# Gated delta-net attention and channel mixing on one core: three steps of the recurrence woven instead of two, heads of four batches exchanged, part of a triangular solve moved to GpSimd

## The reference, cut to what matters

```
q, k = l2norm(silu(conv4(x @ W.T)))        # 16 heads, 64 wide
v    = silu(conv4(x @ Wv.T))               # 16 heads, 128 wide
alpha = exp(-exp(A_log) * softplus(x @ Wa.T + dt_bias)); beta = 2*sigmoid(x @ Wb.T)
for t in range(1024):                      # per batch and head
    S = alpha_t * (S - beta_t * k_t (k_t S)) + k_t v_t
    o_t = S q_t
out = rmsnorm(o) @ Wo.T
```

## Time and profile before

| | |
|---|---|
| median of 3 runs | 4767.3 us (4766.52 to 4771.13) |
| profiled execution | 4768.39 us, its span 4766.6 us |
| mean granted TensorE clock | 0.932 of 2.4 GHz |
| busy in the span | PE 3981.9 us, DVE 3447.9, ACT 2826.5, POOL 1620.0 |
| one engine's list once round (KT of step 0 to KT of step 127, over 127) | 34.67 us |

### The profile page before, as it was taken

How to read it: one execution, slowest core, us unless ns; L and a number is a source line. 1 busy time by engine, 2 the same in 40 slices (tenths; PEclk the granted TensorE clock), 3 DMA queues, 4 the chain that set the end, 5 groups by cost and what they waited for, 6 DMA issues and landing times. The chain is left out here.

```text
span 4766.6 us, 171733 instructions
## 1 busy us (share of the span) xinstructions
PE 3981.9 (84%) x67980; PEld 2818.1 (59%) x67980; DVE 3447.9 (72%) x7448; ACT 2826.5 (59%) x4519; POOL 1620.0 (34%) x1574
## 2 busy tenths in 40 slices
PE   5888888888888888888888888888888888888855
PEld 4565665656666565666666565666656566666644
DVE  5777777777777777777777777777777777777745
ACT  2666656666565656656665666656565665666534
POOL 2333333333333333333333333333333333333311
PEclk9999999999999999999999999999999999999977
DMA  1211111121211112121111111121111212111111
GB/s 53 44 38 42 39 38 41 39 43 39 43 38 40 41 37 42 39 43 38 41 40 37 42 39 43 39 42 38 38 43 37 43 39 43 38 41 40 36 39 40
DMA packets 877987, 191.80 MB, mean 40 GB/s; under 512 B 816000, under 2 KB 873600, under 8 KB 877952
## 3 DMA queue, kind: packets, MB, share of 16 engines
q1 hardware_dynamic: 871648, 173.49, 17.3%
q0 software_dynamic: 6304, 17.84, 1.3%
HBM read 136.16 MB, written 55.06 MB: 40 GB/s over the span
## 5 line engine op out<-in xcount | busy, mean ns | idle before, releaser
L830 DVE SCALAR_TENSOR_TENSOR cv<-ps,w_v,cv 128x512 f32<-128x512 f32 x768 | 576.6, 751 | 562.7 <-ACT cv L695 544.6
L830 DVE SCALAR_TENSOR_TENSOR cv<-ps,w_kq,cv 128x512 f32<-128x512 f32 x768 | 575.2, 749 | 139.9 <-ACT cv L695 121.8
L695 ACT ACTIVATE cv<-ps,w_kq 128x512 f32<-128x512 f32 x256 | 175.9, 687 | 623.0 <-PE ps L449 623.0
L502 PE MATMUL ps<-k_all,KB 64*64 64x64 f32 x4096 | 225.4, 289 | 326.3 <-issue 326.3
L460 PE MATMUL ps<-Lm,k_all 128*128 128x512 f32 x768 | 418.5, 626 | 0.0
L997 POOL TENSOR_TENSOR sq<-sl 128x512 f32<-128x512 f32 x128 | 133.0, 1039 | 838.6 <-ACT sl L710 838.6
L990 POOL COPY stP<-tabP 128x24 f32 (+1 forms) x128 | 25.3, 197 | 1144.1 <-DVE KT L859 1144.1
L502 PEld LDWEIGHTS ps<-k_all,KB 64*64 64x64 f32 x4096 | 206.2, 197 | 340.0 <-issue 340.0
L469 PE MATMUL ps<-sq,k_all 128*128 128x512 f32 x512 | 285.1, 639 | 138.6 <-ACT ex L702 138.6
L710 ACT ACTIVATE sl<-cv 128x512 f32<-128x512 f32 x256 | 161.5, 631 | 369.8 <-DVE cv L830 369.8
L449 PE MATMUL ps<-xnT,w_v 128*128 (+1 forms) x1024 | 298.2, 412 | 98.8 <-DVE Nd L845 53.0
(11 more groups left out here) (184 smaller groups left out, 10890.3 us busy)
## 6 DMA issues: line engine op xcount, KB each, us to landing
scrN<-Nd SPq DMA_DIRECT2D x256, 128.0 KB, 2.4
Z<-scrZ SPq DMA_DIRECT2D x256, 128.0 KB, 2.8
X<-scrX SPq DMA_DIRECT2D x512, 64.0 KB
w_v<-wtab SPq DMA_DIRECT2D x128, 132.0 KB, 2.1
w_kq<-wtab POOLq DMA_DIRECT2D x128, 132.0 KB, 2.4
wo_s<-wo SPq DMA_DIRECT2D x128, 128.0 KB, 2.4
NS<-scrN SPq DMA_DIRECT2D x128, 64.0 KB, 2.5
scrZ<-XT SPq DMA_DIRECT2D x128, 64.0 KB, 2.5
```

Source lines behind the costliest of these rows:

```text
L502: last = nc.tensor.matmul(sub_block(ps, 6 * 512, b, a, z), sub_block(BD["KB"], 0, b, a, z), k_all[a:z, K_ID + a:K_ID + z], start=True, sto ...
L695: nc.scalar.activation(cv4[:, j], pj[:, :, 0:C], ACT.Copy, scale=tap(j, 0)).then_inc(tap0.sem, 1)
L830: nc.vector.scalar_tensor_tensor(cv4[:, j], pj[:, :, k:k + C], tap(j, k), cv4[:, j], ALU.mult, ALU.add).then_inc(conv.sem, 1)
```

## The change

It does these things.

- **Three steps woven.** `body(l, m, n)` with m = l + 1 and n = l + 2: output, state update and second inverse round of l; SiLU of v, inverse and first round, ks and R of m; projections, keys and decay factors of n. There is one more partly filled round at each end.
- **Heads exchanged for batches 4 to 7.** "Class 1" batches keep their token tensors (V, R, U, the decay of the tables) with the two heads' partitions exchanged (`place`, `other`), so that in both Grams, ktr, ks, ds, y, x and z class 0 uses two quadrants and class 1 the other two. u keeps two. The exchange is made in the tables, in `wab` and by the output pattern of the SiLU of v (`sv_out`).
- **Decay factors.** `pe_decay`'s three 128x512 products become eight 64x64x256 ones (`pe_dec`), one exp of 1024 columns writes both factors. exp(g) for all steps is written once, ahead of the steps, to HBM (scrG), and SyncE reads a step's rows repeated over 64 partitions (`sp_g`, two DMAs).
- **Substitution on GpSimd.** `pool_elim`, 14 instructions of up to 32 elements in a row, replaces numbers 0 to 12 of `dve_sub`; VectorE keeps five.
- w_kq is issued by SyncE instead of GpSimd. ScalarE's list changes its function table four times in a round instead of twice. The S part and the U part of o are split by a wait for class 1.

The lists of the round, and what the prediction's steps use:

```diff
-SUBS = 18
+ELIM = 14
+SUBS = 5
+        def sp_g(sp, n):
+            if not first(n):
+                sp.wait_ge(qg_ok.sem, qg_ok.at(n - 1))
+            for h, (a, z) in enumerate(HALF):
+                sp.dma_start(half(ex, 2)[a:z], scrG[bass.ds(n, 1), h, :].to_broadcast([C, NB * C])).then_inc(g_in.sem, 16)
+        def sp_inv_out(sp, n):
+            sp.wait_ge(sub.sem, sub.at(n, SUBS - 1))
+            sp.dma_start(blocks(scrZ), X16).then_inc(z_out.sem, 16)
+            sp.wait_ge(sub.sem, sub.at(n))
+            sp.dma_start(blocks(scrX), XB[0:64, :]...).then_inc(x_out.sem, 16)
+        def sp_body(sp, m, n, q):          # called with (i, i+1, i+2), as the others with (l, m, n)
+            if q is not None:
+                sp_wkq(sp, q)
+            sp_gram(sp, n)
+            if m is not None:
+                sp_wo(sp, m)
+            if q is not None:
+                sp_wv(sp, q)
+                sp_g(sp, q)
+            sp_inv_out(sp, n)
+            sp_inv_in(sp, n)
+        def pool_qg(pool, n):
+            pool.wait_ge(qn_ok.sem, qn_ok.at(n))
+            pool.wait_ge(g_in.sem, g_in.at(n))
+            if not first(n):
+                pool.wait_ge(o_mm.sem, o_mm.at(n - 1))
+            nc.gpsimd.tensor_tensor(half(BD["QG"], 0), qn[:], half(ex, 2), ALU.mult).then_inc(qg_ok.sem, 1)
+        def pool_elim(pool, n):
+            if not first(n):
+                pool.wait_ge(z_out.sem, z_out.at(n - 1))
+                pool.wait_ge(sub.sem, sub.at(n - 1))
+            pool.sem_inc(pool_go.sem, 1)
+            nc.gpsimd.tensor_copy(XT[0:64, 0:256], k_all[0:64, K_XI:K_XI + 256]).then_inc(elim.sem, 1)
+            pool.wait_ge(n_in.sem, n_in.at(n))
+            for k in range(7):
+                r, c = 7 - k, k + 1
+                pool.wait_ge(elim.sem, elim.at(n, max(2 * k, 1)))
...
+                    nc.gpsimd.tensor_tensor(t, NB8[...], XB8[...], ALU.mult).then_inc(elim.sem, 1)
+                    pool.wait_ge(elim.sem, elim.at(n, 2 * k + 1))
+                    nc.gpsimd.tensor_tensor(XB8[:, :, 0:c, c:8], XB8[:, :, 0:c, c:8], t, ALU.add).then_inc(elim.sem, 1)
+        pe_body(l, m, n), with "part(step)":
+            gram_k(m) proj3(m) y1(l) x(l) z1(l) nq(m) u(l) proj0(n) o(l) ds(l) ms(l) ktr(m) proj1(n)
+            gram_p(m) ks(m) vtr(m) nk(n) wo(l) proj2(n) dec(n) y0(m) z0(m)
+        act_body: silu_v0(m) u1(l) tap0_0(n) TABLE nq_ln(m) osq(l) osq(l) nq_exp(m) o_ln, o_exp(l) twice TABLE
+            silu_v1(m) tap0_1(n) silu_k(n) sq_k(n) v(m) nk_max(n) TABLE nk_ln(n) tap0_2(n) nk_exp(n) y0(m)
+            exp(n) TABLE silu_q(n) y1(m) x(m) tap0_3(n) z1(m) nq_max(n) u0(m)
+        dve_body: conv3(m) conv0(n) s(l) s(l) sub 0-3(m) k(m) on(l) on(l) p(m) sub 4(m) conv1(n) r(m) acc(l)
+            conv2(n, two) keys(n) conv2(n, last) z0(m) n(n) str(n)
+        pool_body: qg(l) nm(l) dmn(m) sq_q(m) elim(m) dmp(m) qn(m) stp(n) lm(n) sg(m)
```

More of the change, by code:

```diff
@@ L463, in pe_norm, with pe_dec @@
[L463 to L467, removed]
-                pe.wait_ge(pt_ok.sem, pt_ok.at(n - 1))
-            nc.tensor.matmul(bank((2, 6)[i]), kc(K_BD), half(sq, i), start=True, stop=True).then_inc(nrm_mm.sem, 1)
+        def pe_dec(pe, n):
+            pe.wait_ge(lm_ok.sem, lm_ok.at(n))
+            if not first(n):
+                pe.wait_ge(r_ok.sem, r_ok.at(n - 1))
+            pe.sem_inc(pe_go.sem, 1)
+            for i, o in enumerate((K_LE, K_GT)):
+                for cls in range(2):
+                    for a, z in HALF:
+                        c = (PAIR_C + cls) * 512 + i * 4 * C
+                        last = nc.tensor.matmul(ps[place(cls, a), c:c + 4 * C], k_all[a:z, o + a:o + z],
+                                                Lm[a:z, i * 512 + cls * 4 * C:i * 512 + (cls + 1) * 4 * C], start=True, stop=True)
+            last.then_inc(dec_mm.sem, 1)
@@ L496, in pe_ktr, with pe_vtr @@
             else:
+                pe.wait_ge(nq_mx.sem, nq_mx.at(n))
                 pe.wait_ge(dec_ex.sem, dec_ex.at(n))
-                pe.wait_ge(nrm_mx.sem, nrm_mx.at(n))
             pe.sem_inc(pe_go.sem, 1)
[L500 to L503, removed]
-            last.then_inc(k_tr.sem, 1)
[L506 to L509, removed]
+            for i in range(4):
+                for cls in range(2):
+                    for a, z in HALF:
+                        last = nc.tensor.matmul(ps[place(cls, a), col64(PAIR_C, cls, i)], blk64(BD["KB"], CLASSES[cls][i], a),
+                                                k_all[a:z, K_ID + a:K_ID + z], start=True, stop=True)
+            last.then_inc(k_tr.sem, 1)
+        def pe_vtr(pe, m):
+            pe.wait_ge(silu_v.sem, silu_v.at(m))
+            if not first(m):
+                pe.wait_ge(on_ok.sem, on_ok.at(m - 1))
+            else:
+                pe.wait_ge(g_cp.sem, g_cp.at(0))
             for b in range(NB):
@@ L512, in pe_vtr, with pe_y @@
             last.then_inc(v_tr.sem, 1)
[L515 to L530, removed]
+        def pe_y(pe, m, n, l):
             if l:
-                pe.wait_ge(y_ok.sem, y_ok.at(m, 1))
+                pe.wait_ge(z_ok.sem, z_ok.at(m, 1))
             else:
@@ L558, in pe_z @@
             pe.sem_inc(pe_go.sem, 1)
[L559 to L566, removed]
+            for i in range(4):
+                for cls in range(2):
+                    for a, z in HALF:
+                        b = CLASSES[cls][i]
+                        q = place(cls, a)
+                        last = nc.tensor.matmul(ps[a:z, col64((PAIR_B, PAIR_A)[l], cls, i)],
+                                                BD["X" if l else "X0"][q, b * C:(b + 1) * C],
+                                                BD["Y"][q, b * C:(b + 1) * C], start=True, stop=True)
             last.then_inc(z_mm.sem, 1)
         def pe_ks(pe, m):
-            pe.wait_ge(kb_ok.sem, kb_ok.at(m))
             pe.wait_ge(kt_ok.sem, kt_ok.at(m))
@@ L741, in act_x, with act_v @@
+        def act_v(act, m):
+            act.wait_ge(v_tr.sem, v_tr.at(m))
+            if not first(m):
+                act.wait_ge(r_ok.sem, r_ok.at(m - 1))
+            nc.scalar.activation(Vt[:], bank(PAIR_B, 2), ACT.Copy).then_inc(v_ok.sem, 1)
         def act_x(act, m):
             act.wait_ge(x_mm.sem, x_mm.at(m))
[L743 removed]
+            if not first(m):
+                act.wait_ge(z_mm.sem, z_mm.at(m - 1))
+            nc.scalar.activation(two(half(BD["X"], 0)), pair(PAIR_A), ACT.Copy).then_inc(x_ok.sem, 1)
@@ new lines, in act_u, with act_osq @@
+        def act_u(act, m, g):
+            act.wait_ge(u_mm.sem, u_mm.at(m, g + 1))
+            if first(m):
+                act.wait_ge(g_tr.sem, g_tr.at(0))
+            else:
+                act.wait_ge(ds_mm.sem, ds_mm.at(m - 1))
+            nc.scalar.activation(half(U, g), bank(PAIR_C + g), ACT.Copy).then_inc(u_ok.sem, 1)
+        def act_osq(act, m, h):
+            act.wait_ge(o_mm.sem, o_mm.at(m))
+            if not first(m):
+                act.wait_ge(wo_mm.sem, wo_mm.at(m - 1))
+            nc.scalar.activation(half(oo, h), bank(PAIR_B + h), ACT.Square).then_inc(o_sq.sem, 1)
@@ new lines, in sp_inv_in @@
+        def sp_inv_in(sp, n):
+            sp.wait_ge(z_out.sem, z_out.at(n))
+            if not first(n):
+                sp.wait_ge(u_mm.sem, u_mm.at(n - 1))
+            for h, (a, z) in enumerate(HALF):
+                sp.dma_start(v3(BD["Z"], 0)[a:z], rows(scrZ, h)).then_inc(z_in.sem, 16)
+            sp.wait_ge(x_out.sem, x_out.at(n))
+            if not first(n):
+                sp.wait_ge(x_ok.sem, x_ok.at(n - 1))
+            for h, (a, z) in enumerate(HALF):
+                sp.dma_start(v3(BD["X0"], 0)[a:z, 0:4], rows(scrX, h)[:, 0:4]).then_inc(x_in.sem, 16)
+                sp.dma_start(v3(BD["X0"], 0)[other(a), 4:8], rows(scrX, h)[:, 4:8]).then_inc(x_in.sem, 16)
```

869 lines of the change are left out of this document (473 added, 396 removed).

## The result

| | before | after |
|---|---|---|
| median us | 4766.95 (4766.52 to 4771.13, 4 runs) | 5142.51 (5142.01 to 5142.74, 4 runs) |
| span of the profiled execution | 4766.6 | 5140.9 |
| KT to KT, over 127 | 34.67 | 37.56 |
| outside the 127 rounds | 363.1 | 370.3 |

What follows compares the result with a forecast made beforehand. The prediction took a ring through SyncE's wait for QG as the bound: 34.3 us plus 1.3 for clock and 0.5 for port made 36.1 us a round, 4958 us in all; range 4700 to 5200, forecast's own 4830 to 5110.

Steps and rivals of the forecast that it cites:

- the wait for QG ahead of the store: On SyncE: g loads wait for POOL's QG, holding back the inverse's store; QG ready 6.35 us after KT.
- the ring: Chain of waits across engines closing over one step, from KT's end to the next; 34.3 us before two additions.
- the third rival: Elimination on GpSimd is the bound: 13 small instructions take 8.7 us, total 5182 us; chance 0.15.
- The first rival: SyncE's wait for QG is not last; PE and ACT set a 28.3 us round, total 3967 us; chance 0.05.
- The second rival: TensorE keeps 2.4 GHz, no port conflicts, g loads cost no queue time: round 33.8 us, total 4665 us; chance 0.16.
- the clock: TensorE's clock falls after idling ahead of z0, slowing z0, gram_k and proj3: 1.3 us a round, between 0 and 2.5.
- the port: VectorE's sub 0 may wait for GpSimd's dmp and qn at SBUF: 0.5 us a round, up to 1.27.
- outside the rounds: Work before and after the 127 rounds: exp(g) preparation and a longer last step, +9 us, 0 to 20.
- Terms 1 and 2: From KT's end: POOL's stP, Lm, Sg and QG, 6.35 us, then SyncE issuing two g loads, 0.7 us.
- Terms 3 and 4: From the scrZ issue to X landed for z0, 8.5 us, plus g loads' traffic on the queue, 0.5 us.
- Term 6: Second inverse round, from the end of copy Z to the start of u: 4.9 us.

Runs made afterwards that it cites:

- e1: The changed kernel, but SyncE asks for the exp(g) rows after the inverse's two stores and six loads; 4132.79 us, ratio 0.8674 to the kernel before.
- e2: The changed kernel with SyncE's order kept, but POOL multiplies QG(m) right behind qn(m), not first in its next round; 4161.29 us, ratio 0.8734 to before.
- e7: e1 with POOL's qn(m) made to wait until VectorE's sub 0 to 2 are done; 4045.43 us, ratio 0.8482 to before.
- e8: e7 with VectorE making the transposed copy XB (sub 4) right behind KT(m); 3901.75 us, ratio 0.818 to before.
- e5: The changed kernel with eight unused products added on TensorE, six ahead of y0 and two between y0 and z0; 5047.66 us, ratio 1.0581 to before.
- e4: The changed kernel, but POOL's qn(m) waits until VectorE's sub 0 to 2 are done; 5137.85 us, ratio 1.0783 to before.
- e3: The changed kernel with five unused products added on TensorE between dec(n) and y0(m); 5143.63 us, ratio 1.0795 to before.

## Why the prediction was right, and what its sizes missed

The mechanism was right: the wait for QG ahead of the store closes the ring, and e1 and e2 remove it in two ways. The size was not: it came out at half of the measured one, 191 of 376 us. The measured 5142.5 us lie above the forecast's own 4830 to 5110. They are inside 4700 to 5200 only by the room left for the third rival, the elimination as the bound, and that is not what happened. To that extent the range held by luck.

The first rival, that this wait is not last, is refuted by e1 and e2. Its 28.3 us, the round of PE and ACT alone, is near what is left without the wait (e1 29.62, e7 28.96), but no floor: e8 has 27.81. The second rival failed as the clock fell and the port bit in every one of the 115 rounds. The third failed as the small instructions on GpSimd took 0.20 to 0.26 us and 0.31 apart, 4.0 in all where I had 5.5.

The point was 184 us low: 127 times 1.46 us, less 1.8 us outside the rounds. By the terms, with the round of after shown above:

| stretch | forecast | measured |
|---|---|---|
| 1, 2: KT's end to the scrZ issue | 7.05 | 7.62 |
| 3, 4: to the start of z0 | 9.0 | 8.95 |
| 5: to the end of the copy Z | 1.94 | 2.38 |
| 6: to the start of u | 4.9 | 6.36 |
| 7: to the start of o | 2.95 | 3.01 |
| 8: to the end of S | 4.7 | 4.83 |
| 9: to KT's end | 3.75 | 4.46 |
| on top: clock and port | 1.8 | in 5, 6 and 9 |
| sum | 36.1 | 37.6 |

- **Terms 1 and 2, 0.57 short.** POOL's part was 5.93, less than 6.35. But the two g issues took 1.35, with 0.19 ahead and 0.15 behind, not 0.7. I had priced them by w_v's 0.34 for its long rows; the nearer row was scrZ's at 0.57, 64 partitions as g.
- **Terms 3 and 4** met; over 115 rounds the mean is 9.01. How much of it the g traffic ahead makes stays open. In before, without it, the stretch was 8.68 in the mean of the 15 such rounds in which z0 waited for X, so some 0.3 us of the 0.5 may be it. e2 against e1 doesn't tell, since both wait for XB there.
- **Term 6, 0.55 short beside the clock.** In e1, at full clock, the end of Z to u is 2013.34 - 2007.89 = 5.45, not 4.9. y1 starts 0.62 after Z, since gram_k and proj3 stand ahead of it in PE's list; I had taken 0.1.
- **The clock, 1.3 forecast.** From z0 to u after takes 8.63 us, e1 7.42 and e5, which has after's order and the clock held, 7.43 (means over 115 rounds): 1.2 us. The step is right in size.
- **The port, 0.5 forecast.** The port is what a VectorE instruction with both inputs in SBUF waited for while GpSimd worked. qn started 0.36 ahead of sub 0, and sub 0 took 1.46 at the median, not 0.67 (e4): 0.8. I had weighed two orders; POOL came first in all 115 rounds. POOL was busy for 38% of the span, not for over half as I wrote. The Trainium skill, page "SBUF — State Buffer", section "Who interferes with whom", has the rule that the later of the two waits for the whole instruction. The trace agrees: sub 0 ended 0.55 after qn did, and alone it takes 0.67.
- **Outside the rounds**, 7.2 us more against 9 forecast.
- **The gain on PE** came: both Grams and ktr in 0.69 for 32 instructions at full clock (the earlier trace rows has 1.15 for gram_p, so 0.46 less and not 0.3), ks and ds in 1.10 and 1.08 with the drain (the earlier trace rows has 1.96 for ds), and the decay product in 1.09. Of all this only ds is on the ring while the wait stands.

What stays open: what each part of the change (three steps woven, heads exchanged, exp(g) by DMA, the shorter form of the elimination) brings of e1's 13.3%. Only the elimination's engine was tried alone. On e1 and e8 it makes 0.3% at most, and those were run on different chips, so that nothing follows from so little.

## What to carry to other kernels

A list in program order is a chain of waits: before a wait is put on a queue, ask what is queued behind it and where the awaited item stands in its own engine's list, the next round included. Here a prefetch that nobody needed for a whole round stood ahead of a store on the ring, and cost more than the rest of the change gained. When an edit that plainly shortens an instruction on the ring moves nothing, compare the round stretch by stretch: if another one has become longer at low clock, try the edit once with the clock held. The mean granted clock doesn't tell what the clock costs (e3); where in the round it is low does.

## What the runs showed that was not expected

Three kernels had the same round: after 37.56, e3 (4901.2 - 129.1) / 127 = 37.58 and e4 37.56 us, while TensorE's clock fell and came back once in each of the 115 rounds. For e3 this is plain: from z0 to u it takes 8.69 us, after 8.63, as the clock is low there in both. For e4 two stretches changed by 0.77 and 0.80 us and cancelled. Why they come so near to each other was not tested.

A copy of 64x256 on VectorE, with one input, took 1.07 to 1.08 us while GpSimd ran Lm or Sg (after, e1) and 0.36 where it began ahead of them (e8). Moved ahead of the three instructions that stood between KT and it, together with X landing sooner, it was worth 144 us.
